# A four-layer attention and expert kernel: first scores ahead of the first value turns, bias addition behind the first value table

## The reference

```
def _L0_xattn_ref(query, key, value, mask, Wq, bq, Wk, bk, Wv, bv, Wo, bo):
    B, S, D, H = (4, 256, 128, 16)
    DK = D // H
    q = _split_heads(query @ Wq + bq)
    k = _split_heads(key @ Wk + bk)
    v = _split_heads(value @ Wv + bv)
    scale = 1.0 / jnp.sqrt(jnp.asarray(DK, dtype=q.dtype))
    scores = jnp.einsum('bhqd,bhkd->bhqk', q, k) * scale
    scores = scores + mask * -1000000000.0
    attn = jax.nn.softmax(scores, axis=-1)
    x = jnp.einsum('bhqk,bhkd->bhqd', attn, v)
    x = x.transpose(0, 2, 1, 3).reshape(query.shape[0], -1, D)
    return x @ Wo + bo
...
x = x + _L0_xattn_ref(_layernorm(x, axis=-1), ctx_1024, ctx_1024, mask_1x1xSxS2_fk1, L0_xattn_Wq, ...)
```

## Time and profile before

| | us |
|---|---|
| median of 3 runs | 876.34 |
| lowest and highest run | 875.88, 879.57 |
| span of the profiled execution | 877.9 |
| TensorE busy in it | 757.7 |
| VectorE, ScalarE, GpSimd busy | 538.3, 518.1, 291.1 |

### The profile page before, as it was taken

One profiled execution on the slowest core, in us unless ns is written; L12 is line 12 of the kernel. 1 busy time (PEld: TensorE's weight loads), 2 busy tenths in 40 slices (PEclk: granted clock), 3 DMA queues, 4 the chain that ended last, 5 costly groups with the idle time before them and its releaser, 6 DMA issues.

```text
span 877.9 us, 15816 instructions
## 1 busy us (share of the span) xinstructions
PE 757.7 (86%) x4663; PEld 616.2 (70%) x4663; DVE 538.3 (61%) x1919; ACT 518.1 (59%) x1751; POOL 291.1 (33%) x334
## 2 busy tenths in 40 slices
PE   3888878788888898899999899989999998876597
PEld 1566657666666477677997577778778875665597
DVE  4756657444454779765555897776233056886575
ACT  1878666345554888764556555568553348773275
POOL 4200031353552333543352344442000013243355
PEclk9999989868999999999999999999999999897599
DMA  7894477023324320000313890000000050000121
GB/s 234 211 205 196 121 222 162 28 87 81 83 62 121 147 73 1 14 13 27 80 49 121 208 214 15 1 1 1 1 0 1 1 187 6 1 16 10 50 70 50
DMA packets 35956, 69.57 MB, mean 79 GB/s; under 512 B 7121, under 2 KB 25809, under 8 KB 32033
## 3 DMA queue, kind: packets, MB, share of 16 engines
q1 hardware_dynamic: 30384, 57.98, 24.4%
q0 software_dynamic: 4768, 9.91, 3.3%
q10 hardware_dynamic: 720, 0.68, 0.3%
HBM read 58.45 MB, written 37.67 MB: 109 GB/s over the span
## 4 chain that ended last, share of the span: by engine, by line
PE 52%; DVE 17%; ACT 12%; issue 9%; POOL 6%; DMA 1%; another core or an unknown queue 1%; SPq 1%; POOLq 0%; DVEq 0%; ACTq 0%
PE bank L1226 10%; PE bank L1063 6%; PE bank L1094 6%; PE bank L1198 5%; ACT s_S L1892 4%; PE bank L1022 4%; PE bank L1077 3%; DVE s_xn L1388 3%; POOL out L2089 3%; PE bank L1092 3%; PE bank L1177 3%; PE bank L1171 2%; POOL xs_L L2082 2%; DVE s_peak L1425 2%; ACT s_S L1895 2%
## 5 line engine op out<-in xcount | busy, mean ns | idle before, releaser
L1063 PE MATMUL bank<-s_A,s_xTq 128*128 128x462 f32 (+1 forms) x352 | 149.1, 520 | 5.5 <-ACT s_S L1895 1.7
L2055 POOL TENSOR_TENSOR s_S<-s_S,s_inv 128x462 f32<-128x462 f32 (+2 forms) x123 | 100.4, 834 | 141.8 <-DVE s_inv L1439 140.2
L1077 PEld LDWEIGHTS bank<-s_ident,s_S 128*128 128x128 f32 (+2 forms) x560 | 67.9, 144 | 74.9 <-issue 39.2
L1077 PE MATMUL bank<-s_ident,s_S 128*128 128x128 f32 (+2 forms) x560 | 91.5, 284 | 26.7 <-POOL s_S L2055 11.8
L1915 ACT ACTIVATE s_PT<-bank 128x384 f32<-128x384 f32 (+1 forms) x176 | 82.6, 478 | 43.7 <-PE bank L1077 39.2
L1094 PE MATMUL bank<-s_VW,s_PT 128*128 128x128 f32 (+2 forms) x800 | 100.9, 282 | 0.0
L2082 POOL DMA_INDIRECT xs_L<-s_xn,s_sli x64 | 62.2, 971 | 116.2 <-DVE s_sli L1546 75.2
L1094 PEld LDWEIGHTS bank<-s_VW,s_PT 128*128 128x128 f32 (+2 forms) x800 | 96.9, 199 | 0.0
L1892 ACT ACTIVATE s_S<-s_S,s_peak 128x77 f32<-128x77 f32 x256 | 67.7, 351 | 7.0 <-DVE s_peak L1425 6.5
L1063 PEld LDWEIGHTS bank<-s_A,s_xTq 128*128 128x128 f32 x352 | 57.1, 199 | 17.4 <-issue 7.9
L1962 ACT ACTIVATE s_hT<-bank,s_b1T 128x128 f32<-128x128 f32 x184 | 52.3, 369 | 21.8 <-issue 9.1
(11 more groups left out here) (234 smaller groups left out, 1674.2 us busy)
## 6 DMA issues: line engine op xcount, KB each, us to landing
xs_L<-xs_L SPq DMA_DIRECT2D x24, 1122.0 KB, 30.9
s_xe<-xs_L SPq DMA_DIRECT2D x85, 66.0 KB
s_moe<-in_L_w SPq DMA_DIRECT2D x2, 2048.0 KB, 10.4
s_moe<-in_L_w SPq DMA_DIRECT2D x8, 512.0 KB, 7.4
s_yb<-ys_L SPq DMA_DIRECT2D x12, 256.0 KB, 3.0
s_arena<-in_L_w SPq DMA_DIRECT2D x2, 1024.0 KB, 6.1
s_arena<-in_L_h SPq DMA_DIRECT2D x2, 1024.0 KB, 9.2
s_b2bc<-in_L_b SPq DMA_DIRECT2D x2, 512.0 KB, 24.3
```

The costliest lines, as they stand in the source:

```text
L1063: mm(bank[b][:, 0:(h1 - h0) * KEYS], xTq_of(L, n)[:, i % 4, :], A[:, n, h0 * KEYS:h1 * KEYS], start=True, stop=True).then_inc(scores.up(L, ...
L1077: w = turn(bank[b][0:m, P * (t - t0):P * (t - t0) + P], S[s][:, P * t:P * t + m], ident)
L2055: p.tensor_tensor(val, val, rep(inv[s][:, h0:h1], KEYS, 2), ALU.mult).then_inc(normed.up(L, i, k), 1)
```

## The change

Three things are rewritten in make_plan. The bias addition xb 0 is put behind vbd 0 instead of in front of it. The first two score pieces, S 0 0 0 and S 0 0 1, are put ahead of vbd 0 and of the first turns vw0 0 q, and are no longer given by first_order. Since tick runs once for each score piece that first_order gives, two ticks fewer have passed at every later place of layer 0, so that the side pieces stand later among the score pieces, by one or two places, until the side lists meet at fixed points (from the eighth tile on the list is as it was).

```
@@ first_order
         now, nxt = s < NT, s + 1 < NT
         out = []
-        if s == 0:
-            out += [("S", 0, 0, 0), ("S", 0, 0, 1)]
         if now:
             out += [("S", 0, s, 2)]
@@ make_plan
     put("k0")
     put("v0")
-    woven(before(0, 0), [])
+    for piece in before(0, 0):
+        if not isinstance(piece, int) and piece[0] != "xb":
+            put(*piece)
     def values(n):
         out = [("a0", n), 5] if n else []
-        out += [("vbd", n), 6]
+        out += [("vbd", n), *[("xb", 0)] * (n == 0), 6]
         for q in range(len(spans(0))):
             out += [("vw0", n, q), 3]
         return out
 
     put("a0", 0)
+    put("S", 0, 0, 0)
+    put("S", 0, 0, 1)
     woven(values(0), [])
```

## The result

| | us |
|---|---|
| before, median of 7 runs | 877.35 |
| before, lowest and highest | 875.76, 879.57 |
| after, median of 7 runs | 881.12 |
| after, lowest and highest | 879.35, 882.87 |
| after against before | 1.0046 (95%: 1.0031 to 1.0060) |

The change costs 0.46%, about 4.0 us. That is inside the half per cent that the prediction calls hard to tell from no change, but the interval is clear of 1. It is above the whole range of the prediction (874.2 to 879.8).

What follows compares the result with a forecast made beforehand. ScalarE was taken to bound the kernel from 26.84 to 46.6 us, then mostly TensorE. Terms +0.7 - 0.3 - 0.4 = 0.0 us left the span at 877.9, or 876.3 us against the median, range 874.2 to 879.8.

Steps and rivals of the forecast that it cites:

- +1.0 was taken: First norm on VectorE: its variance waits for GpSimd's value table and ends 1.0 us later, bounds 0 and 1.3.
- fast turns: First value table's turns on TensorE at the faster clock level, some 3.5 us with copies; the forecast's case, 0.45.
- norm pair: ScalarE: two instructions of the second group's norm leave idle time and stand behind the first six exponentials, +0.4 us.
- late maxima: Fourth tile: VectorE's maxima come some 0.2 us late for ScalarE, which starts earlier, +0.2 us.
- Wq product uncovered: Second group's product with Wq, 1.12 us, no longer covered by the fourth tile's exponentials; with two handovers +1.2 us.
- slow turns: Rival: first turns and copies stay at TensorE's slower level, 4.8 us; price +1.3 us, 877.6 us; chance 0.2.
- Wo wait: First product with Wo on TensorE: its 0.67 us wait at 54.07 us for a copy of turned values goes, -0.3.
- 0.39 was allowed for: Turns behind the first product with Wo wait for the addition to x, as at 69.89 us, 0.39 us.
- I take 25.7: ScalarE's first exponential starts at 25.7 us, 1.1 earlier, behind scores ending at 22.2 and 3.5 us of turns.
- third rival: Longer pause before the fifth tile's scores keeps TensorE's clock slow longer: 1.6 us more, 879.2 with slow turns; chance 0.15.
- doubles in length: TensorE's half-clock stretch behind the fifth tile's scores, already costing 1.6 us, becomes twice as long, costing 1.6 more.
- The rival's argument against: Against a longer slow clock: once TensorE works without a break, the slow level was over by 50.4 us.

Runs made afterwards that it cites:

- e1: After with the two missing ticks given back, so scores and table stay moved and only the weaving is as before: 878.08 us, ratio to before 0.9996.
- e2: After with the first value table on GpSimd held back until the normed rows are there: 879.46 us, ratio to before 1.0027.
- e6: The changed kernel itself, unaltered, run again on a second chip: 852.11 us, ratio to before 1.0049.
- e7: Before with only the two scores ahead of the turns and the shifted weaving, bias addition where it was: 851.73 us, ratio to before 1.0009.
- e4: Before with two neighbours exchanged, the turn of the second group's rows now behind the fourth tile's exponentials: 880.33 us, ratio to before 1.0036.
- e9: The same kernel as e4, run again on a third chip: 851.61 us, ratio to before 1.0022.
- e3: Before with only the bias addition put behind the first value table: 875.46 us, ratio to before 0.9985.
- e8: Before with the bias addition behind the first value table and that table waiting for the normed rows: 849.61 us, ratio to before 0.9987.

## Why the prediction was wrong

**The start, point by point.** The table ran from 9.76 us, and the variance was held to its end: +1.15 us, +1.0 was taken. Statistics and aggregation were not held. The Trainium skill, page "SBUF — State Buffer", section "SBUF: two separate sides", has the exclusive pair taken, on VectorE's side, only by instructions in a two-port mode or with two SBUF inputs. By that rule one instruction can be held and the next not, and the trace agrees: 1.32 us for the variance, 0.38 for the aggregations beside the same table. Which mode they ran in no row here shows. The scores began at 19.03 (19.1). The turns with their copies took from 22.27 to 26.88 us, 4.6: the forecast's fast turns (3.5) failed, and the rival's 4.8 was near. The scores just before did not give them the faster level in this execution. It differs from run to run: of the five profiles with the scores ahead, e1, e2 and e6 ran the second and third part of the turns at the faster level (from the first turn to the last copy's end 3.7 to 3.9 us), after and e7 did not (4.6); of the nine with the turns ahead none did.

**Up to the fifth tile's scores.** The terms, as measured: first exponential +0.04 (26.88), norm pair +0.4, late maxima +0.15, Wq product uncovered +1.22; sum +1.81, and the trace has 48.54 - 46.67 = +1.87. With the slow turns the prediction had said +2.0. The whole start of after's execution was 0.26 us earlier (the first variance at 10.73, not 10.99), so that +2.1 is the fairer number. So the list of instructions was read rightly.

**Behind it.** The Wo wait went, as forecast, and 0.47 us for x came instead (0.39 was allowed for). With the slow turns the prediction's sum is +1.3 us; at the fourth product with Wo this pair of profiles has +1.8, counted from the first variance, with equally long slow stretches in both. That is near, but the runs say 4.0.

**The two steps that failed.** The first is *"I take 25.7"*, the fast turns: the first exponential came 1.2 us later, at 26.88. The second is *"Uncovered, with two handovers of 0.05 us, it is +1.2"*: the product was priced at its length, and the clock behind it at nothing. e4, which does that exchange alone, cost +2.7 ± 1.2 us, and e9 +2.75 ± 2.5; filled, the exchange is 1.2 to 1.5 us in the traces, so that the length was right. The rest of the price is, as far as the traces show, the clock. The two steps make 1.2 + 1.5 = 2.7 us of the miss; the remaining 1.3 lie within the intervals. Where the product is uncovered, TensorE stands still for 2.07 to 2.34 us, works 1.1 (1.7 in e4), stands 0.8, and a half-clock stretch lies there in 6 of 6 profiles. Where it is covered, such a stretch was there in 1 of 4.

**The baseline.** That one is the very profile from which the prediction was made. The earlier trace rows showed 1.6 us lost at the slow level (1.7 by the table above), and the prediction took it as always there, so that the change could only lengthen it. In the three other profiles with the covered product and no filling (e1, e3, e8) it is not there. The third rival came nearest. With the slow turns it has +2.9 where +4.0 was measured, by the ratio's interval 2.7 to 5.3, and it names the pause. But its mechanism is not the one seen in the changed kernel: the stretch *"doubles in length"* in e4 and e9 (6.8 us), while in after and e6 it is as long as in before (3.4 us). What the change seems to alter is how often there is one. The rival's argument against, that the slow level ends once TensorE works without a break, tells how long a stretch is, not how often it comes.

**What is shown and what is not.** Shown: the loss lies in the shifted weaving (gone in e1), and the exchange of one pair alone makes a loss of its size (e4). Made likely but not shown by the runs: that the clock is a good part of it, and that before has the slow stretch only in a share of its executions. The traces show it going with the filling; the times do not tell filled from unfilled. Open: whether the changed kernel loses 1 us more than e4. The intervals (+3.6 ± 1.6 and +2.8 ± 2.2 against +2.7 ± 1.2 and +2.75 ± 2.5) do not tell. Nor do the parts add up to the whole: bias addition behind -2.0 ± 1.2, scores ahead with the weaving +1.9 ± 2.0. In both the first exponential comes 1.0 to 1.7 us earlier; in after it does not. For that the traces have the reason. With the turns ahead the held norm costs nothing, since they run while xTq is still being made (e3). With the scores ahead, which need xTq, it moves all that follows: the scores start at 19.03 and not 18.03 as in e7, the first exponential at 26.88 and not 25.88, and with the norm free again (e2, where the later turns were fast, too) it is at 25.09.

## What to carry to other kernels

When side work is woven in by counting pieces, taking a piece out of the count shifts all that is woven behind it; look for products and copies that hid beside a neighbour and now do not. Price a pause of TensorE at its length and, besides, the chance of a half-clock stretch behind it (1.7 us each here, by one pair of traces), and see whether the profile that you start from happens to have such a stretch already. And look where the profiled execution stands among the runs before comparing two spans: here it was the slowest against the fastest.

## What was unexpected in the hardware

**Chips differ by 3%.** The same kernel took 877.55 us on one chip and 850.09 and 849.45 on two others, each chip in a group of runs of its own, at the same granted clock in most slices. Part of it shows in the expert stage (line L2091 writes finished rows indirectly, from GpSimd). First the changed kernel's main profile, then its repetition e6:

```profile
228.94 0.96 POOL L2091 DMA_INDIRECT ys_L<-s_yo,s_yi  x1 [1.49 <-DVE s_yo L1661]
230.21 0.96 POOL L2091 DMA_INDIRECT ys_L<-s_yb,s_yi  x1 [0.30 <-issue]
231.47 0.96 POOL L2091 DMA_INDIRECT ys_L<-s_yb,s_yi  x1 [0.30 <-issue]
233.94 0.96 POOL L2091 DMA_INDIRECT ys_L<-s_yb,s_yi  x1 [1.51 <-DVE s_yb L1661]
```

```profile
227.98 0.96 POOL L2091 DMA_INDIRECT ys_L<-s_yb,s_yi  x1 [0.30 <-issue]
229.24 0.96 POOL L2091 DMA_INDIRECT ys_L<-s_yb,s_yi  x1 [0.30 <-issue]
230.51 0.96 POOL L2091 DMA_INDIRECT ys_L<-s_yb,s_yi  x1 [0.30 <-issue]
231.77 0.95 POOL L2091 DMA_INDIRECT ys_L<-s_yb,s_yi  x1 [0.30 <-issue]
```

Three writes take 5.0 us on the one and 3.8 on the other (steps of 1.26), though each instruction takes 0.96 on both. In the slower one every third write waits some 1.5 us for VectorE, which waits for TensorE, which waits for ScalarE's copies. What starts that circle was not looked into.

**GpSimd and VectorE slow each other down both ways.** The bias addition took 3.67 us beside the key tables and 1.27 with nothing beside it; the value table 4.64 beside them (e8) and 2.26 alone; the variance 1.32 instead of 0.17. By the dates the later one mostly waited for the earlier to end. In before the key tables end at 16.07 us and the bias addition at 17.20, in e8 they end at 16.00 and the value table at 18.12: 1.13 and 2.12 us behind them, a little under what each takes alone. VectorE's statistics and aggregations were not held.
